# A two-layer adaptive FFN kernel on one core: half of the first projection in fp16 passes, a shorter warm-up, and vector work moved

## The reference

```python
x = x + L0_ffn(L0_cond(x, cond_8, weight, mask, bias), router_w, expert_weights)
x = x + L1_ffn(L1_cond(x, cond_8, W_base, b_base, As, Bs), gate_w, exp_*, sh_*)
# L0_cond: w[b] = sum_g cond_8[b,g]*weight[g]*mask;  h = x @ w[b].T + bias
# L0_ffn:  probs = softmax(h @ router_w.T); the top 2 of 8 experts; per token
#          sum of w_k * (h @ E_k + prob_k), w_k = prob_k / (sum of both + 1e-6)
# L1_cond: h = x @ W_base.T + b_base + 2 * low-rank part weighted by cond_8
# L1_ffn:  2 shared experts (all tokens) + top 2 of 8 routed experts,
#          each silu(h @ g) * (h @ u) @ d, inner width 352
```

## Time and profile before

| | |
|---|---|
| median of 3 runs | 354.28 us (354.05 to 354.62) |
| the profiled execution | 354.84 us |
| its span in the trace | 353.1 us |
| PE busy | 346.8 us, 98% |
| DVE / ACT / POOL busy | 239.1 / 172.5 / 147.8 us |

### The profile page before, as it was taken

The page is one execution under the profiler, slowest core; times in us unless marked ns, Lnnn a source line. Parts: engine busy times, 40 slices in busy tenths (PEclk is TensorE's granted clock), DMA queues, the critical chain, the costliest instruction groups (busy, mean ns, idle before and its releaser), DMA issues.

```text
span 353.1 us, 8015 instructions
## 1 busy us (share of the span) xinstructions
PE 346.8 (98%) x2746; PEld 216.9 (61%) x2747; DVE 239.1 (68%) x618; ACT 172.5 (49%) x296; POOL 147.8 (42%) x252
## 2 busy tenths in 40 slices
PE   8999999999999999999999999999999999999996
PEld 4444444454455454566458777777777777766655
DVE  1369899997766754789985555555555565655696
ACT  1178468558558648544541333333333333424493
POOL 4049475656646644000012355555555555422000
PEclk9999999999999999999999999999999999999999
DMA  7976122442343321010005334444454353111963
GB/s 275 407 305 218 59 100 81 159 159 91 129 156 85 136 80 61 0 61 0 2 1 187 113 132 162 174 146 156 138 177 163 132 156 119 61 46 49 351 226 119
DMA packets 20505, 47.42 MB, mean 134 GB/s; under 512 B 2432, under 2 KB 11392, under 8 KB 20480
## 3 DMA queue, kind: packets, MB, share of 16 engines
q1 hardware_dynamic: 17024, 37.65, 29.9%
q0 software_dynamic: 3456, 9.44, 8.4%
HBM read 29.25 MB, written 8.91 MB: 108 GB/s over the span
## 4 chain that ended last, share of the span: by engine, by line
PE 81%; DVE 13%; ACT 3%; issue 3%; DVEq 0%; ACTq 0%
PE bank L1156 58%; PE bank L1167 7%; PE bank L1330 4%; PE bank L1433 4%; PE bank L1408 2%; DVE x L863 2%; PE bank L1182 2%; DVE prod L1045 2%; DVE yg L959 1%; ACT w1s L658 1%; ACT sil L669 1%; DVE acts L1053 1%; PE bank L1172 1%; PE bank L1246 1%; PE bank L1257 1%
## 5 line engine op out<-in xcount | busy, mean ns | idle before, releaser
L1156 PE MATMUL bank<-w0s,hs 128*128 128x512 f16 x384 | 86.5, 379 | 0.9 <-DVE x L863 0.9
L513 POOL TENSOR_TENSOR w1s<-piece,w1s 128x170 f16<-128x170 f32 x128 | 60.9, 514 | 42.4 <-ACT piece L600 42.4
L522 POOL DMA_INDIRECT rows<-token_store,row_in x36 | 35.0, 971 | 77.7 <-DVE row_in L990 45.3
L863 DVE SCALAR_TENSOR_TENSOR x<-bank,coef,x 128x256 f32<-128x256 f32 x128 | 54.4, 476 | 14.2 <-PE bank L1156 14.1
L1156 PEld LDWEIGHTS bank<-w0s,hs 128*128 128x128 f16 x384 | 37.1, 98 | 42.9 <-DVE x L863 1.4
L1156 PE MATMUL bank<-hs,w1s 128*128 128x512 f16 x264 | 59.4, 379 | 0.3 <-DVE prod L1045 0.2
L1156 PE MATMUL bank<-w1s,rT 128*128 x336 | 54.5, 313 | 0.0
L528 POOL DMA_INDIRECT results<-yb,row_out x36 | 35.7, 992 | 35.9 <-ACT yb L707 35.9
L701 ACT ACTIVATE ract<-prod 128x352 f16<-128x352 f32 x36 | 17.9, 497 | 53.9 <-DVE prod L1128 44.0
L1156 PEld LDWEIGHTS bank<-hs,w1s 128*128 128x128 f16 x264 | 25.3, 98 | 29.2 <-DVE prod L1045 1.3
L1156 PEld LDWEIGHTS bank<-w1s,rT 128*128 128x128 f16 x336 | 31.7, 98 | 14.7 <-issue 0.2
(11 more groups left out here) (183 smaller groups left out, 498.4 us busy)
## 6 DMA issues: line engine op xcount, KB each, us to landing
piece<-w SPq DMA_DIRECT2D x16, 680.0 KB, 4.0
xrow<-w1s SPq DMA_DIRECT2D x8, 704.0 KB, 3.6
xrow<-w1s SPq DMA_DIRECT2D x8, 384.0 KB, 3.0
w1s<-results SPq DMA_DIRECT2D x6, 512.0 KB, 10.0
x<-wc SPq DMA_DIRECT2D x4, 512.0 KB, 5.0
w1s<-xT SPq DMA_DIRECT2D x4, 512.0 KB, 9.7
w1s<-w SPq DMA_DIRECT2D x4, 512.0 KB, 9.1
x<-x SPq DMA_DIRECT2D x4, 512.0 KB, 8.4
```

What stands on the lines that cost most here:

```text
L513: ins = nc.gpsimd.tensor_tensor(w1s[:, LO, at], piece[:, i % 2, part], w1s[:, HI, at], ALU.subtract)
L522: pool.indirect_dma_start(rows[:, i % 2], None, token_store, bass.IndirectOffsetOnAxis(row_in[:, slot_tile(i):slot_tile(i) + 1], 0)).then_ ...
L863: nc.vector.scalar_tensor_tensor(x1[:, t], bank[(n + a) % 4][:, h * D:(h + 1) * D], coef[:, t, e:e + 1], x1[:, t], ALU.mult, ALU.add).then ...
L1156: mm = nc.tensor.matmul(out_ap, l, r, start=(i == 0), stop=(i == len(terms) - 1))
```

## The change

- `FILL` is 4 in place of 14.
- Batches 2 and 3 (`HALVED`) are projected by `project0_16`: three fp16 passes for each of the 4 fp32 products. ACT rounds `wacc` of both batches and x of batch 3, DVE rounds x of batch 2 and makes all four low halves. PE waits for `s_xlo2`/`s_xlo3` and `s_walo`.
- On ACT `w0_scaled(0)` stands ahead of `h_hi(0, 1)`, `w0_scaled(1)` ahead of `exps(0)`.
- `shares0` loses one instruction (the scale goes into coef) and a link; its last four instructions are now `bias0`, called after j = 1 of m = 0 for the first part. `h_lo(0, 2)` comes before `second` and `shares0`; on PE `logits(0, 2)` and `logits(0, 3)` come one j later.
- 12 of the 32 `hot_lanes` instructions run on POOL (`s_slots`, `s_lanes`), after the last weight piece.
- `shares1` moves from the last routed tiles into `accumulate(1)`, a piece per tile; DVE's loop over the routed tiles is one pair longer.
- PE transposes the rows of routed tile 2 in step -1 instead of step 0.

```diff
-    FILL = 14
+    FILL = 4
...
+            pool.wait_ge(sm["s_pclo"], NP)
+            pool.wait_ge(sm["s_slots"], 1)
+            for n in range(5 * ENTRIES // 8, ENTRIES):
+                ins = nc.gpsimd.tensor_scalar(hot_lo[:, n], lane16[:], slot_lo[:, n:n + 1], None, ALU.is_equal)
+            ins.then_inc(sm["s_lanes"], 1)
...
+            for n, c in enumerate(HALVED):
+                act.wait_ge(sm["s_wacc"], c + 1)
+                nc.scalar.activation(wacc16[c][:, HI], wacc[:, c], ACT.Copy).then_inc(sm["s_wahi"], 1)
             h_hi(0, 0)
             w0_hi(0)
+            w0_scaled(0)
             h_hi(0, 1)
-            w0_scaled(0)
+            act.wait_ge(s_xin[3], 16)
+            nc.scalar.activation(x16[3][:, HI], x_in[3], ACT.Copy).then_inc(sm["s_xhi3"], 1)
             w0_hi(1)
+            w0_scaled(1)
             exps(0, PARTS[0], 1.0 / (SH0 * SW))
-            w0_scaled(1)
             h_hi(0, 2)
...
             h_lo(0, 0)
+            dve.wait_ge(s_xin[2], 16)
+            nc.vector.tensor_copy(x16[2][:, HI], x_in[2]).then_inc(sm["s_xhi2"], 1)
+            dve.wait_ge(sm["s_xhi2"], 1)
+            nc.vector.tensor_tensor(x16[2][:, LO], x_in[2], x16[2][:, HI], ALU.subtract).then_inc(sm["s_xlo2"], 1)
...
             h_lo(0, 1)
+            dve.wait_ge(sm["s_xhi3"], 1)
+            nc.vector.tensor_tensor(x16[3][:, LO], x_in[3], x16[3][:, HI], ALU.subtract).then_inc(sm["s_xlo3"], 1)
             largest(PARTS[0])
+            h_lo(0, 2)
             second(PARTS[0])
             shares0(0, PARTS[0])
-            h_lo(0, 2)
...
+                    if m == 0 and j == 1:
+                        bias0(PARTS[0])
...
+            def project0_16(c):
+                for o in range(KT):
+                    i = c * KT + o
+                    if i >= 6:
+                        pe.wait_ge(sm["s_hlo"], i - 5)
+                    group(h_bank(i)[:], [(wacc16[c][:, a, k * D + o * P:k * D + (o + 1) * P], x16[c][:, b, k])
+                                         for k in range(KT) for a, b in PASSES], "s_h")
...
+                if known(i) and again(i) and not (isinstance(s, int) and s == 0):
+                    turn_rows(i, par)
+                if isinstance(s, int) and s == -1:
+                    turn_rows(2, 0)
```

More of the change, by code:

```diff
@@ L199, in build_program @@
                 .rearrange("p (k w) -> p k w", k=KT) for hl in range(2) for n in range(2)]
+        x16 = {c: w1s[:, c % 2, 0:2 * KT * S].rearrange("p (a k n) -> p a k n", a=2, k=KT) for c in HALVED}
+        wacc16 = {c: w1s[:, c % 2, 2 * KT * S:2 * KT * S + 2 * KT * D].rearrange("p (a n) -> p a n", a=2) for c in HALVED}
         YW = 2 * K_TOP * TPB * D
@@ L222, in build_program @@
             "s_wacc",
+            "s_wahi",
+            "s_walo",
+            "s_xhi2",
+            "s_xlo2",
+            "s_xhi3",
+            "s_xlo3",
             "s_rsp",
@@ L367, in landed, with run_tiles @@
             return i * 8 + (16 - 8 * par)
-        def run_tiles(eng, step, ahead, beside=None):
+        def run_tiles(eng, step, ahead):
             for s in range(-2, 3):
@@ L378, in run_tiles @@
                 step(s, s % 2)
-                if beside is not None:
-                    beside(s)
         @block.sync
@@ L760, in _ @@
                 masked(b)
+            for n, c in enumerate(HALVED):
+                dve.wait_ge(sm["s_wahi"], n + 1)
+                nc.vector.tensor_tensor(wacc16[c][:, LO], wacc[:, c], wacc16[c][:, HI],
+                                        ALU.subtract).then_inc(sm["s_walo"], 1)
             h_lo(0, 0)
+            dve.wait_ge(s_xin[2], 16)
+            nc.vector.tensor_copy(x16[2][:, HI], x_in[2]).then_inc(sm["s_xhi2"], 1)
+            dve.wait_ge(sm["s_xhi2"], 1)
+            nc.vector.tensor_tensor(x16[2][:, LO], x_in[2], x16[2][:, HI], ALU.subtract).then_inc(sm["s_xlo2"], 1)
             def each(a, tiles):
@@ L799, in shares0, with bias0 @@
                 link(nc.vector.reciprocal(REC[:, tiles], S2[:, tiles]))
-                link(nc.vector.tensor_scalar(REC[:, tiles], REC[:, tiles], 1.0 / (SH0 * SW), None, ALU.mult))
-                link(nc.vector.tensor_tensor(coef[:, tiles], t1[:, tiles], each(REC, tiles), ALU.mult))
+                link(nc.vector.scalar_tensor_tensor(coef[:, tiles], t1[:, tiles], 1.0 / (SH0 * SW), each(REC, tiles),
+                                                    ALU.mult, ALU.mult))
+            def bias0(tiles):
                 link(nc.vector.tensor_tensor(t1[:, tiles], t1[:, tiles], coef[:, tiles], ALU.mult))
@@ L875, in _ @@
                         shares0((m + 1) // 2, PARTS[(m + 1) // 2])
+                        bias0(PARTS[(m + 1) // 2])
                     if j == 0 and m >= 3 and m % 2 == 1:
@@ L891, in _, with shares1 @@
                     second(PARTS[m // 2 + 1])
-            def shares1(s):
-                if s == TILES - 5:
+            def shares1(q):
+                if q == 0:
                     dve.wait_ge(sm["s_exp"], 4)
@@ L1068, in accumulate @@
                     t = c * TPB + q
-                    if c == 0:
+                    if c == 0 and q < 2:
                         hot_lanes(2 * q)
-                        if q < TPB - 1:
-                            hot_lanes(2 * q + 1)
+                        hot_lanes(2 * q + 1)
+                    if c == 0 and q == 2:
+                        hot_lanes(2 * q)
                     if c == 1 and q == TPB - 2:
@@ L1077, in accumulate @@
                                                    ALU.mult, ALU.add).then_inc(sm["s_acc"], 1)
+                    if c == 1:
+                        shares1(q)
                     if c == 2 and q == 1:
@@ L1135, in _ @@
             dve.wait_ge(sm["s_ahi"], EARLY)
-            run_tiles(dve, step, 4, shares1)
+            run_tiles(dve, step, 2)
             step(TILES, TILES % 2)
@@ L1285, in _ @@
                         lora(LORA[m])
-                    if m == 0 and j < 2:
-                        logits(0, 2 + j)
+                    if m == 0 and j in (1, 2):
+                        logits(0, 1 + j)
                     if j == 1 and m >= 1:
@@ L1398, in _, with turn_rows @@
                     down(DOWN[i])
+            def turn_rows(i, par):
+                pe.wait_ge(s_row[par], landed(i, par))
+                for a in range(2):
+                    for k in range(KT):
+                        o = (a * KT + k) * P
+                        mm = nc.tensor.transpose(bank16[4][:, o:o + P], rows[:, par, o:o + P], ident16[:])
+                mm.then_inc(sm["s_ra"], 1)
             def step(s, par, down_at, gate_at, down_own=None, gate_own=None):
@@ L1402, in step @@
                 i = s + 2
-                if known(i) and again(i):
-                    pe.wait_ge(s_row[par], landed(i, par))
-                    for a in range(2):
-                        for k in range(KT):
-                            o = (a * KT + k) * P
-                            mm = nc.tensor.transpose(bank16[4][:, o:o + P], rows[:, par, o:o + P], ident16[:])
-                    mm.then_inc(sm["s_ra"], 1)
+                if known(i) and again(i) and not (isinstance(s, int) and s == 0):
+                    turn_rows(i, par)
+                if isinstance(s, int) and s == -1:
+                    turn_rows(2, 0)
                 i = s - 1
```

33 lines of the change are left out of this document (22 added, 11 removed).

## The result

| | before | after |
|---|---|---|
| median of 6 runs | 354.45 us | 351.62 us |
| all runs | 353.88 to 355.40 | 351.27 to 352.13 |
| profiled execution, span | 354.84, 353.1 us | 351.79, 350.1 us |
| PE / DVE / ACT / POOL busy | 346.8 / 239.1 / 172.5 / 147.8 | 343.4 / 239.2 / 174.8 / 157.2 |

A forecast was written before the change was run, and what follows sets the result against it. PE, busy 98%, was taken as the bound, with DVE's full queue a second one between 21 and 46 us; -0.6 - 0.4 - 0.3 + 0.3 - 0.6 = -1.6 gave 352.7 us median (353.2 profiled), range 351.2 to 353.9.

The forecast's parts named there:

- Step 1: Start of PE: ten fewer warming products, clock rising at the same moment; -0.6 us, ends 0 and -1.2.
- Step 2: Projections of batches 2 and 3: fp16 passes take 1.9 us off PE; conversions costed at nothing for batch 2.
- Step 3: DVE's full queue before 46 us: of 2.5 us gained on PE only -0.6 booked, ends 0 and -2.5.
- relief of the small instructions: DVE queue before the first sum: small two-input instructions run faster in holes of POOL's work; about -0.25 us.
- Step 4: PE's second wait on DVE's sums, near 55 us: shares0 of tiles 4 to 7 gets shorter; -0.4, ends 0 and -0.6.
- Step 5: Lane tables: twelve instructions of 0.17 us leave DVE for POOL; -0.3, ends 0 and -0.6.
- rival D: POOL's lane tables block DVE for all their 5.2 us, PE 3.1 later; 356.1 us, 5%.
- Step 6: Tile 2's transposes one step earlier: PE waits 0.75 for the row DMA, not 0.43; +0.3, ends -0.4 and +0.8.
- Step 7: Last routed tiles: with shares1 gone, copies PE needs are no longer held back; -0.6, ends -0.3 and -0.6.
- A: Rival: DVE's queue holds nothing back, so PE's early gains pass whole and its waits go; -4.0, 350.3 us, 8%.
- B: Rival: DVE's queue holds everything back, small instructions stay slow, ACT comes later; -0.7 or less, 353.6 to 353.9, 16%.
- C: Rival: with fewer warming products the clock stays low into the mix; up to 359.3 us if throughout, 6%.

The follow-up runs named there:

- fp32 run: Changed kernel with all four batches projected in fp32 again, without the conversions for batches 2 and 3; ratio 0.9945 to the kernel before.
- POOL-quiet run: Changed kernel with 28 of POOL's 32 subtractions for low halves of layer 0 weights replaced by a zero fill; ratio 0.9902 to the kernel before.
- run with the term first: Changed kernel with the additive term (bias0) of tiles 0 to 3 back ahead of the first sums; ratio 0.9905 to the kernel before.
- split search: Changed kernel, tile 2 transposes mid-step -1, second-expert search of tiles 4 to 7 behind m = 1's first sums, additive term behind its last; 0.9887 to kernel before.
- 14 small products: Changed kernel with 14 small warming products back in place of 4; ratio 0.9913 to the kernel before, on a slower, scattering chip.
- x of batch 3 on POOL: Changed kernel with batch 3's x rounded by DVE, its low half made by POOL, batch 2's low half behind the second-expert search; 0.9960 to kernel before.
- transposes in step 0: Changed kernel with the transposes of tile 2's rows back in step 0; ratio 0.9918 to the kernel before, on a slower, scattering chip.

## Why the prediction was right, and where it was not

The direction and the range were right; the gain was 2.8 us where I had 1.6. Against the profiled executions the sum misses by 1.4. Its terms up to the shared experts miss by 1.7, and the transposes go 0.3 the other way.

The mechanism was right in kind and too strong in size. Of the signs that I had named, three did not come. The first sum was to stand within 0.5 us of 30.80 and stands 1.36 before it. PE's waits on the sums were to grow to over 2 us and are 1.2. The first products of the mix were to be twice as far apart, and in this trace they are not (0.46 and 0.43 us for eight records).

- **Step 1, ten warming products: right for the work, lucky in this pair.** I took -0.6 with the rise at the same moment. The work is 0.55. The other half of the -1.11 is that the level rose near 5.2 in this trace and near 6.3 in the one before, and no run shows that the products caused it. They also take 1.08 and not 1.21 from the start of the mix: the 1.70 for the 14 have the modelled end of the last in them.
- **Step 2, fp16 passes: right, but for 0.1.** They took 1.9 from PE (2.75 and 2.76 us each), and 1.72 of it reached the start of the expert loop. The conversions weren't free: the subtraction for x of batch 3 ends at 22.66, and PE's second fp16 projection starts at 22.72, 0.12 later than it would by the usual distance.
- **Step 3, the full queue: right in kind, too small in size.** DVE is the second bound, and the fp32 run shows that of 1.9 us only 0.46 come through. But my sum for the first sum gave 30.7 and it stands at 29.44. The terms: the start 0.5 earlier than booked (step 1); the relief of the small instructions, which I took as 0.25. The small instructions from the first search up to the first sum took 6.93 us before and take 4.68 now (22.57 to 24.17 and 26.36 to 29.44). 1.4 of the difference I had booked as `bias0` and the dropped instruction, so 0.84 is relief, 0.6 more than my term. (Before, they stood between 22.55 and 29.48 in the timeline of DVE.) I had priced the disturbance from one pair, 0.35 against 0.19, and the relief as holes in POOL's work. The one hole, from 26.4 to 27.7, is worth 0.54: three two-input instructions in it took 0.47, 0.35 and 0.29 before. The rest came beside a busy POOL, where the loss is whatever is left of POOL's instruction, and depends on how the two queues happen to lie. That part was not forecast and could have gone the other way. The wait for ACT was 0.87, not 1.0. The POOL-quiet run bears this out: even the changed kernel has 0.35 left to give. Behind the first sum 0.2 more came than the 0.44 that I had from idle time and `bias0` (with the 0.1 ahead of it they make 0.54, where I booked 0.6). In all -2.0 at 46 us instead of -0.6.
- **`bias0` as a gain of its own: wrong.** Its -1.1 stood in my sum for the first sum and +0.8 behind it. The run with the term first shows 0.05 for the two together, where I had 0.3.
- **Step 4, the second wait: right.** 0.5 against 0.4 at 55 us. Another 0.2 went at 81 us, at a wait for low-rank weights which I had not listed.
- **Step 5, lane tables: right in size.** B fell by 0.32 against 0.3. POOL needs 0.67 us for each of the twelve, not the 0.43 of rival D, and DVE's own grew from 0.174 to 0.19 or 0.2, but D's blocking did not come. That B is due to the lane tables alone was not tried apart.
- **Step 6, the rows: right.** +0.57 in the profiled execution, +0.3 on average, the number forecast, and for the reason given: the wait of 0.75 was 0.73.
- **Step 7, the shares: right.** -0.60 in D, and undone by putting them back.

Step 1 and the relief of step 3 account for 1.1 of the 1.7 us that I missed at the front (-2.69 in the first two rows of the table of stretches against -1.0), 0.2 each behind the first sum and at 81 us for 0.4, and the wait for ACT and step 4 for the rest.

Of the rivals, A came nearest, and for the front it came nearer than the forecast: -2.69 was measured, A had -3.4, the forecast -1.0. The 351.6 lie about midway between the 352.7 of the forecast and the 350.3 of A. A fell short because PE still waits 1.2 at 44 us, and the fp32 run shows that of 1.9 us on PE only 0.46 come through. B fell. C fell: the level rose by some 7.1 us even in the worst of twelve traces with 4 small products. D fell: during the lane tables DVE's instructions took 0.02 to 0.03 us more each. But my argument against it, that small instructions lose 0.16 and not a whole instruction of POOL, read the rows wrongly. The lock that I cited from the Trainium skill (SBUF — State Buffer, Who interferes with whom) for D is there: the page has the second to issue fully blocked for the whole instruction where DVE is in a 2-port mode. The trace shows as much for instructions with two inputs: POOL waited through DVE's subtraction (1.48 us in place of 0.43), and DVE's small ones waited for the rest of POOL's, up to 0.33.

## What to carry to other kernels

Before adding up what an edit takes from the busiest engine, find the stretch where the next engine has no idle time: there a saving on the first is worth little (0.46 of 1.9 us here), and so is an order on the second (0.05 for the additive term, 0.38 for the split search). Work taken off the second counts only if nothing fills its place: the subtraction moved to POOL came back as longer small instructions, and of 0.35 us won with POOL quiet 0.2 arrived at PE. A block in such a queue may be the cover of something on a third engine; ask what arrives during it before moving it. Where runs scatter by more than the edit is worth, compare distances between fixed points of one engine's timeline: they repeated within 0.1 us here where ratios could not tell 0.5.

## What the runs showed of the hardware that was not expected

- **The moment at which TensorE's clock rises differs between executions of the same code,** from 4.1 us, while the wide warming products still ran, to some 7.1 us (the mix of 8.02), and moves the first projection, and all behind it, between 11.86 and 13.14. The granted clock in the windows reads 1.00 before the rise as well; it is the rate of the products that tells.
- **Of two overlapping instructions on DVE and POOL that each read two inputs from SBUF, the later waits for the earlier.** On DVE a small one took 0.19 us in all of the 14 traces where POOL was idle. Beside POOL it took 0.19 to 0.52. All 119 of 32 columns that took over 0.20 us, in the 14 traces between 20 and 62 us, end 0.05 us behind an instruction of POOL. POOL's took 1.48 and 1.41 in place of 0.43 (the changed kernel, x of batch 3 on POOL) where a subtraction of 1.2 us on DVE had begun just before it. Reductions took 0.19 either way, and the sums with one input from PSUM (L897) 0.47 to 0.49 either way. A copy of 1024 columns, with one input, took 0.87 beside POOL in place of 0.68.
- **On one chip the loop over the routed tiles stopped now and then.** In the trace with 14 small products PE was 1.0 to 1.1 us late three times, at 225.5, 254.1 and 282.8, always at the same place of the program; in the ten traces of other chips D shows none. DVE had waited there for nothing that the profile names:

```profile
224.73 0.42 DVE L1156 COPY aT<-bank 128x256 f32<-128x256 f32 x1 [1.76 <-remote]
```

The four traces of that chip (14 small products, fp32 projections, transposes in step 0, x of batch 3 on POOL) had three, two, three and three of them, of 0.4 to 1.1 us, which fits the slower and scattered times there. What the engines waited for stays open.
